# Relation messages added by indirect DMA onto two arrays of sums in DRAM, in place of a target sum stage

## The chip, the core and the metric

The kernel runs on one core of a Trainium2 chip. Its engines work side by side: PE (TensorE: matmuls, and PEld, its weight loads), DVE (VectorE), ACT (ScalarE), POOL (GpSimd) and SP (SyncE, which here only issues DMAs). Each takes its own instructions in order and waits on semaphores that others raise. The metric is the device time of one execution in microseconds (us), the median of three runs.

## The reference

Four graph layers on the same 1250 nodes (768 features, fp32) and 20000 edges, each followed by a residual sum and a layer norm. The first is three graph attentions side by side and an output product W_out, the second a convolution, the third an attention layer. The change touches the fourth: each edge has one of 34 relations, the rows of the sources are averaged by relation and target, multiplied by the relation's matrix and summed by target; a root product and a convolution follow.

```python
seg = edge_type * n + dst
agg = jax.ops.segment_sum(x[src], seg, num_segments=N_REL * n)
cnt = jax.ops.segment_sum(ones, seg, num_segments=N_REL * n)
mean = agg.reshape(N_REL, n, -1) / jnp.maximum(cnt, 1.0).reshape(N_REL, n, 1)
h1 = jnp.einsum('rni,rio->no', mean, W_rel) + x @ W_root + b_rgcn
xw = h1 @ W_gcn
...
out = jax.ops.segment_sum(xw[src] * norm[:, None], dst, num_segments=n)
out = out + xw * (dinv * dinv)[:, None]
return out + b_gcn
```

Below, the key of an edge is target x 34 + relation: edges of one key go to the same row of `mean`.

## The kernel before

Nodes are held as 10 tiles of 128 rows (1250 of 1280 used), features as 6 pieces of 128. The stages, in order of time:

- **Phase 1** (0 to about 620): x1 = relu(x W_ah), then the three products for attention. Beside it DVE counts the edges' places by prefix sums (PREFIX, with two matmuls on PE for the offsets), and POOL scatters edge records into DRAM by 320 indirect DMAs of 125 records (`scatter`, L767): 160 into dstrec_d, sorted by target, 160 into relrec_d, sorted by relation. A target record has four words, a relation record two (source, key). The target records are read back as `drec`, the relation records as `relrec`. The counts by target and key are made from `drec` with L800.
- **First attention** (att0), then the **W_OUT stage** (about 1101 to 1360): three products of 768x768, one for each third of W_out, each over ten tiles. For a tile PE turns the rows (6 transpositions), ACT copies them (`take`), DVE makes the low part (`low_rows`, L406), PE does 36 matmuls (L298), DVE adds the product to the sum (the z-add, L1443). Fp32 numbers are split in a high and a low part, three products for one. In the third of these products the first norm runs with it.
- Convolution, heads, second attention, W_ROOT (the root product into `hbuf`, the array of h1).
- **Relation stage** (2160 to 3475): the edges, sorted by relation and padded to tiles of 128, make RT = 190 tiles. Functions `pool_rel`, `pe_rel`, `act_rel`, `dve_rel`. For tile k POOL gathers 128 source rows from DRAM into `ct` (L1860), PE turns them (L1886: 6 transpositions against the identity), ACT copies them twice (`take`), POOL subtracts for the low part (L1865), PE multiplies by the relation's matrix (L1898: 36 matmuls of 128x384), ACT empties the product with a scale by 1/count (L1935) and stores it to `msg_d` (L1938). PE stands two turns ahead of the products. DVE splits the next relation's matrix (L1835, L1836) as soon as the last tile of the relation before is done.
- **Target sum stage** (3475 to 3746; `pool_sum`, `pe_sum`, `dve_sum`): POOL gathers the messages from `msg_d` by the target records, four tiles to a group, 49 groups (L1979); DVE makes a one-hot matrix of the targets, PE multiplies by it (L1992), DVE adds into the tile of `hbuf` (L2015). All engines meet before and after it.
- **conv3** (3746 to 3938): h1 W_gcn (turn L324, products L298 again), then the aggregation over the graph.

Nothing reorders the work: each engine's order is the order in which its function issues, the stages are called one after the other in the block of each engine, and SP, ACT and POOL each have queues of DMAs that they issue in that order.

## Time and profile before

| | us |
|---|---|
| median of three runs | 3945.08 (3943.74 to 3946.8) |
| span of the profiled execution | 3937.5 |
| W_OUT stage, first and second third, 20 z-adds | 133.6 |
| relation stage | 1315.2 |
| target sum stage with its meets | 270.8 |

The profiled execution was recorded by the hardware profiler; its span is the time from the first to the last record, and what lies around it in a run's time is not in the trace. A stretch in the views is a window of the span. The granted clock is TensorE's, as a share of full speed (2.4 GHz; 0.50 is 1.2 GHz). PE is busy for 92% of the span, but a stage may be bound by something else; so the stages are to be read apart.

### The profile page before, as it was taken

What the parts mean: (1) busy time and instruction counts of PE and PEld (TensorE: products, weight loads), DVE (VectorE), ACT (ScalarE), POOL (GpSimd) and SP (SyncE); (2) the same over time, 40 slices, a digit from 0 to 9 for tenths busy, and PEclk for the clock granted to TensorE, in tenths of its full rate; (3) what the DMA queues carried; (4) which work ended last, traced back from release to release, by engine and by line L of the source; (5) the groups of instructions that cost most, each with busy time, mean ns of one, the idle gap of its engine ahead of it and who ended that gap; (6) DMA issues with size and microseconds to landing.
All of it is one profiled execution on the core that took longest, in us unless ns stands there. A gap on an engine that the chain in (4) does not pass through costs nothing.

```text
span 3937.5 us, 58219 instructions
## 1 busy us (share of the span) xinstructions
PE 3619.1 (92%) x18463; PEld 2965.8 (75%) x18473; DVE 1958.2 (50%) x2783; ACT 1683.3 (43%) x2911; POOL 1555.4 (40%) x1168
## 2 busy tenths in 40 slices
PE   8998868999988897589989999999999999989998
PEld 4555437999978897333335999999999999965588
DVE  7245788888533635899955333332233331013334
ACT  1113677888832321499981333333333333300021
POOL 3887886666600101000001444444444444357600
PEclk9999998999989998799999999999999999999999
DMA  4343212232232302311014555555555553368901
GB/s 144 90 125 74 46 20 63 74 95 74 78 115 90 123 28 81 108 50 40 34 50 144 198 184 184 173 177 186 184 184 189 179 170 133 112 237 302 284 22 67
DMA packets 176460, 483.10 MB, mean 123 GB/s; under 512 B 40798, under 2 KB 57205, under 8 KB 176342
## 3 DMA queue, kind: packets, MB, share of 16 engines
q1 hardware_dynamic: 87414, 201.95, 15.7%
q0 software_dynamic: 54368, 185.24, 15.2%
q10 hardware_dynamic: 34560, 94.45, 6.8%
q8 instruction: 60, 0.98, 0.1%
q14 instruction: 58, 0.48, 0.0%
HBM read 357.64 MB, written 123.55 MB: 122 GB/s over the span
## 4 chain that ended last, share of the span: by engine, by line
PE 40%; ACT 7%; POOL 5%; issue 3%; DVE 2%; DMA 1%; SPq 0%; POOLq 0%; DVEq 0%; ACTq 0%
PE ps L1898 30%; POOL work L1979 5%; ACT work L1279 4%; PE ps L1886 3%; ACT ps L1270 3%; PE ps L1562 3%; PE ps L306 2%; PE ps L298 1%; DVE work L1101 1%; PE ps L1216 1%; DVE work L1129 0%; ACT work L1289 0%; DMA ct<-x_d 0%; DMA work<-msg_d,ct 0%; PE ps L324 0%
## 5 line engine op out<-in xcount | busy, mean ns | idle before, releaser
L1898 PE MATMUL ps<-wsplit,xsplit 128*128 x6840 | 1238.3, 337 | 2.7 <-DVEq L1838 2.7
L1898 PEld LDWEIGHTS ps<-wsplit,xsplit 128*128 128x128 f32 x6840 | 1182.9, 188 | 2.9 <-issue 2.9
L1835 DVE CAST wsplit<-wplain 128x768 fp32r<-128x768 f32 x204 | 117.3, 575 | 760.8 <-PE ps L1898 745.4
L1865 POOL TENSOR_TENSOR xsplit<-ct,xsplit 128x768 fp32r<-128x768 f32 x190 | 369.3, 1944 | 296.2 <-ACTq L1930 296.2
L1279 ACT ACTIVATE work<-ps,work 128x418 f32<-128x418 f32 x720 | 438.6, 632 | 108.5 <-PE ps L1189 103.2
L1935 ACT ACTIVATE ct<-ps,invs 128x768 f32<-128x768 f32 x190 | 171.5, 902 | 714.3 <-PE ps L1898 714.3
L1226 PE MATMUL ps<-hbuf,work 128*128 128x193 f32 x2400 | 455.8, 328 | 14.8 <-DVE work L1143 13.1
L1226 PEld LDWEIGHTS ps<-hbuf,work 128*128 128x128 f32 x2400 | 408.0, 190 | 42.8 <-issue 16.9
L1270 ACT ACTIVATE ps<-work,lr 128x418 f32<-128x418 f32 x720 | 431.8, 634 | 6.0 <-DMA work<-lrow_d 6.0
L1129 DVE SCALAR_TENSOR_TENSOR work<-work,cnt 128x1250 f32<-128x1250 f32 x240 | 350.0, 1459 | 133.5 <-ACT work L1279 132.8
L1860 POOL DMA_INDIRECT ct<-x_d,relrec x190 | 201.1, 1059 | 457.8 <-PE ps L1886 450.2
L1216 PE MATMUL ps<-work,hbuf 128*65 128x512 f32 x720 | 323.5, 532 | 37.6 <-DVE work L1129 35.8
L298 PE MATMUL ps<-wsplit,xsplit 128*128 128x384 f32 x1800 | 335.7, 344 | 13.1 <-DVE xsplit L406 11.8
L298 PEld LDWEIGHTS ps<-wsplit,xsplit 128*128 128x128 f32 x1800 | 321.2, 194 | 15.5 <-issue 7.5
L1323 POOL DMA_INDIRECT invs<-inv_d,relrec x190 | 281.3, 1480 | 60.0 <-issue 57.6
L1189 PE MATMUL ps<-work 128*128 128x418 bf16 x720 | 247.6, 345 | 31.2 <-DMA work<-shift_d 26.8
L1992 PE MATMUL ps<-work 128*128 128x384 f32 x784 | 257.1, 490 | 12.5 <-DMA work<-msg_d,ct 12.1
L767 POOL DMA_INDIRECT relrec_d<-work x160 | 238.9, 1493 | 48.8 <-issue 48.8
L1836 DVE TENSOR_TENSOR wsplit<-wplain,wsplit 128x768 fp32r<-128x768 f32 x204 | 246.1, 1206 | 7.1
L767 POOL DMA_INDIRECT dstrec_d<-work x160 | 206.0, 1287 | 97.6 <-DVEq L688 49.1
L1992 PEld LDWEIGHTS ps<-work 128*128 128x128 f32 x784 | 149.0, 191 | 120.3 <-issue 15.1
L1796 POOL DMA_DIRECT2D x_d<-work x10 | 5.4, 542 | 565.5 <-DVEq L1761 565.5
(212 smaller groups left out, 4380.5 us busy)
## 6 DMA issues: line engine op xcount, KB each, us to landing
wplain<-in_L_gnn_W_rel SPq DMA_DIRECT2D x34, 2304.0 KB, 9.7
msg_d<-ct ACTq DMA_DIRECT2D x190, 384.0 KB, 2.6
work<-lrow_d SPq DMA_DIRECT2D x47, 625.0 KB, 3.7
feat_d<-work ACTq DMA_DIRECT2D x30, 386.0 KB, 4.1
hbuf<-feat_d SPq DMA_DIRECT2D x60, 193.0 KB, 2.5
gat_d<-work POOLq DMA_DIRECT2D x12, 960.0 KB, 5.2
xplain<-gat_d SPq DMA_DIRECT2D x30, 384.0 KB, 3.1
work<-xa_d SPq DMA_DIRECT2D x27, 384.0 KB, 3.3
```

Of the source, the lines that this page charges most:

```text
L298: last = pe.matmul(ps[:, 4 + 2 * u + h, 0:HALF], x[:, u, c * P:(c + 1) * P], w[:, c * D + h * HALF:c * D + (h + 1) * HALF], start=(q == 0 ...
L767: g.indirect_dma_start(out=(relrec_d, dstrec_d)[which], out_offset=bass.IndirectOffsetOnAxis(addr[:, which, t:t + 1], 0), in_=(relpay[:, t ...
L1129: v.scalar_tensor_tensor(p[:, 0:N], p[:, 0:N], 1.0, cnt3[:, q % NT, 0:N], ALU.min, ALU.mult).then_inc(self.s_p, 1)
L1189: pe.matmul(ps[:, b, 0:c1 - c0], self.ones128, self.crow[h % 2][:, c0:c1], start=False, stop=True, skip_group_check=True).then_inc(self.s_ ...
L1216: last = pe.matmul(ps[0:C + 1, 3 + k, 0:n1 - n0], self.feat(h, s), p[:, n0:n1], start=(s == 0), stop=(s == NT - 1))
L1226: last = pe.matmul(ps[:, self.b0 + b, t * (C + 1):(t + 1) * (C + 1)], p[:, dt * P:(dt + 1) * P], self.feat(h, s), start=(s == 0 and t == 0 ...
L1270: act.activation(ps[:, b, 0:c1 - c0], self.Rb[h % 2][:, c0:c1], ACT.Relu, bias=lr[:, col:col + 1]).then_inc(self.s_relu, 1)
L1279: act.activation(self.p[q % 3][:, c0:c1], ps[:, b, 0:c1 - c0], ACT.Exp, bias=self.l2[:, col:col + 1], scale=1.0 - SLOPE)\
L1323: g.indirect_dma_start(out=invs[:, k:k + 1], out_offset=None, in_=inv_d, in_offset=bass.IndirectOffsetOnAxis(relrec[:, 2 * k + 1:2 * k + 2 ...
L1865: g.tensor_tensor(xlo7[:, k % XW, :], xt7[:, k % 2].rearrange("p c n -> p (c n)"), xhi7[:, k % XW, :].bitcast(F32), ALU.subtract).then_inc ...
L1898: last = pe.matmul(ps[:, 4 + 2 * (u % 2) + h, 0:HALF], x[:, u, c * P:(c + 1) * P], w[:, bass.ds(base + (c * D + h * HALF), HALF)], start=( ...
L1992: last = pe.matmul(ps[:, 2 * (u % 2) + h, 0:HALF], sel8[:, GT * (u % 2) + w, :], mg8[:, GT * u + w, h * HALF:(h + 1) * HALF], start=(w == ...
```

## The change

The messages no longer go to DRAM to be gathered again. Each tile of 128 messages is added by an indirect DMA, with the targets as indices and an addition at the destination, onto one of two arrays of sums in DRAM: acc_d[0] begins as the root product, acc_d[1] as zeros; even tiles go to the one, odd tiles to the other. Two edges of one tile with the same key may not both be added by one DMA; therefore the turn of a tile multiplies by a matrix of equal keys (1 where two rows have the same key) in place of the identity, so that each such row holds the sum, and of equal rows all but one are sent to a spare row behind the nodes (`target`, third word of the relation record). Which rows have an equal key behind them is found in 48 rounds of four tiles in the W_OUT stage: POOL compares the keys of a tile with the keys of all its rows and multiplies by the triangle, DVE reduces and writes the target. In the relation stage POOL makes the equality matrix once more for each tile.

```diff
         def pool_same(g, step):
+            def load(b):
+                g.dma_start(key_rows[:, b % 2, :], key_batch(b)).then_inc(s_keyin0[b % 2], 16)
...
+            for b in range(KEY_BATCHES):
+                k0, k1 = batch(b)
+                if b:
+                    g.wait_ge(s_later, b)
+                if k1 < RT:
+                    load(b + 1)
+                g.wait_ge(s_keyin0[b % 2], 16 * (b // 2 + 1))
+                for w in range(k1 - k0):
+                    step.count(g.tensor_scalar(same0[:, w, :], key_rows[:, b % 2, w * P:(w + 1) * P], keys[:, k0 + w:k0 + w + 1], None, ALU.is_equal))
+                step.wait()
+                found = same0[:, 0:k1 - k0, :]
+                g.tensor_tensor(found, found, tri[:, :].unsqueeze(1).to_broadcast([P, k1 - k0, P]), ALU.mult).then_inc(s_same0, 1)
+
+        def dve_target(v, step, b):
+            k0, k1 = batch(b)
+            later, target = small[:, 48:48 + k1 - k0], rel3[:, k0:k1, 2]
+            v.wait_ge(s_same0, b + 1)
+            step(v.tensor_reduce(later, same0[:, 0:k1 - k0, :], AX, ALU.max))
+            v.sem_inc(s_later, 1)
+            step(v.scalar_tensor_tensor(target, later, dummy_row, target, ALU.mult, ALU.max))
+
+        TARGETS = {(l, j): 3 if j < 6 else 2 for l in range(2) for j in range(NT) if l or j}
...
         def dve_wout(v, step):
                     if j + 2 < NT:
                         d.low_rows(v, (j + 2) // 2, j % 2)
+                    for b in TARGET_OF.get((l, j), ()):
+                        dve_target(v, step, b)
...
         def pool_rel(g, step):
+            def equal(k):
+                b, w = divmod(k, KB)
+                if w == 0:
+                    g.wait_ge(s_keyin[b % 2], 16 * (b // 2 + 1))
+                if k >= GW:
+                    g.wait_ge(s_turn7, k - GW + 1)
+                g.tensor_scalar(same7[k % GW], key_rows[:, b % 2, w * P:(w + 1) * P], keys[:, k:k + 1], None, ALU.is_equal).then_inc(s_same7, 1)
+
+            def add(k):
+                g.wait_ge(s_msg7, k + 1)
+                g.indirect_dma_start(out=acc_d[k % 2], out_offset=bass.IndirectOffsetOnAxis(relrec[:, REC * k + 2:REC * k + 3], 0),
+                                     in_=msg7[:, k % 2, :], in_offset=None, compute_op=ALU.add).then_inc(s_msgst[k % 2], 16)
...
+            for j in range(NT):
+                g.wait_ge(W_ROOT.emptied, W_ROOT.b["emptied"] + j + 3)
+                g.dma_start(acc_d[0][j * P:(j + 1) * P, :], hbuf[:, j * D:(j + 1) * D]).then_inc(s_acc0, 16)
+            g.wait_ge(s_acc0, 16 * NT)
             for k in range(RT):
                 if k + GW < RT:
                     gather(k + GW)
+                if k + 2 < RT:
+                    equal(k + 2)
+                if k >= 3:
+                    add(k - 3)
                 low(k)
...
         def pe_rel(pe):
                 for c in range(KC):
-                    last = pe.transpose(ps[:, 2 * (u % 2) + c // 3, (c % 3) * P:(c % 3 + 1) * P], rows7[:, u % GW, 0, c * P:(c + 1) * P], ident[:, :])
+                    last = pe.matmul(ps[:, 2 * (u % 2) + c // 3, (c % 3) * P:(c % 3 + 1) * P], rows7[:, u % GW, 0, c * P:(c + 1) * P],
+                                     same7[u % GW], start=True, stop=True)
...
         def act_rel(act, step):
                 act.wait_ge(s_prod7, k + 3)
-                act.wait_ge(s_msgst[u % 2], 16 * stores)
+                if stores is not None:
+                    act.wait_ge(s_msgst[u % 2], 16 * stores)
...
-                act.dma_start(msg_d[bass.ds(k * P, P), :], msg7[:, u % 2, :]).then_inc(s_msgst[u % 2], 16)
+                act.sem_inc(s_msg7, 1)
```

At the end of the relation stage SP waits until all adds have landed and loads the two arrays of sums tile by tile, two tiles in flight; DVE adds them (`dve_h1`) into `hbuf`, and conv3's turn of a tile waits for that. `pool_sum`, `pe_sum`, `dve_sum` and their two meets are gone. W_gcn is loaded and split as a 35th matrix of the relations. In phase 1 the relation record gets its third word, the target record loses its fourth, the prefix sums by target come first and the target records are scattered first (their addresses are raised on their own), SP clears acc_d[1] and the spare rows with three DMAs (4.7 MB) from a cleared `ct`, and ahead of the W_OUT stage PE turns the keys, and ACT stores them as rows (`pe_keys`, `act_keys`).

On PE, at the start of the relation stage: `ct` holds the gathered rows, `ident` the identity, L1886 is the turn. Before:

```order
L306 MATMUL ps<-mask,ct 128x384 x24
L1886 MATMUL ps<-ident,ct 128x128 x12
L1907 UNCONDITIONAL_BRANCH
L1907 ISA
L1884 ISA
L1886 MATMUL ps<-ident,ct 128x128 x6
```

and now, where L2057 is the turn (its matrix of equal keys lies in `xplain` or `ct`):

```order
L310 MATMUL ps<-mask,ct 128x384 x24
L2057 MATMUL ps<-xplain,ct 128x128 x12
L2079 UNCONDITIONAL_BRANCH
L2079 ISA
L2053 ISA
L2055 REGISTER_ALU
L2057 MATMUL ps<-ct 128x128 x6
```

The six calls of a turn stand where they stood; the operand ident is replaced.

On DVE, at the first tiles of the W_OUT stage (L1443 the z-add, L406 the low rows; in brackets the semaphores waited for). Before:

```order
L1427 RECIPROCAL dinv<-dinv 128x10 [waits degree_roots]
L1443 TENSOR_TENSOR hbuf<-ps,hbuf 128x768 [waits dense_product,wout_bias_in,dve_step]
L406 TENSOR_TENSOR xsplit<-xplain,xsplit 128x768 [waits dve_step,dense_product,dense_taken]
L1443 TENSOR_TENSOR hbuf<-ps,hbuf 128x768 [waits dense_product,wout_bias_in]
L406 TENSOR_TENSOR xsplit<-xplain,xsplit 128x768 [waits dve_step,dense_product,dense_taken]
```

and now (L1545 the z-add, L410 the low rows, L1409 and L1411 a round's end):

```order
L1545 TENSOR_TENSOR hbuf<-ps,hbuf 128x768 [waits dense_product,wout_bias_in]
L410 TENSOR_TENSOR xsplit<-xplain,xsplit 128x768 [waits dve_step,dense_product,dense_taken]
L1409 TENSOR_REDUCE small<-xplain 128x4 [waits equal_keys_marked]
L1411 SCALAR_TENSOR_TENSOR relrec<-small,relrec 128x4 [waits dve_step]
L1409 TENSOR_REDUCE small<-xplain 128x4 [waits equal_keys_marked,dve_step]
L1411 SCALAR_TENSOR_TENSOR relrec<-small,relrec 128x4 [waits dve_step]
L1409 TENSOR_REDUCE small<-xplain 128x4 [waits equal_keys_marked,dve_step]
L1411 SCALAR_TENSOR_TENSOR relrec<-small,relrec 128x4 [waits dve_step]
L1545 TENSOR_TENSOR hbuf<-ps,hbuf 128x768 [waits dense_product,wout_bias_in,dve_step]
L410 TENSOR_TENSOR xsplit<-xplain,xsplit 128x768 [waits dve_step,dense_product,dense_taken]
```

Three rounds now stand between the low rows of a tile and the z-add of the next.

On POOL, inside the relation stage, one tile before (L1860 the gather, L1865 the low part) and the round ahead of the products in the W_OUT stage, which had nothing:

```order
L1860 DMA ct<-x_d,relrec 128x768 x3
L1860 DMA ct<-x_d,relrec 128x768 [waits turned7]
L1865 TENSOR_TENSOR xsplit<-ct,xsplit 128x768 [waits taken7]
L1860 DMA ct<-x_d,relrec 128x768 [waits turned7]
L1865 TENSOR_TENSOR xsplit<-ct,xsplit 128x768 [waits taken7]
```

and now a tile of the relation stage (L1998 the gather, L2014 the compare, L2020 the add, L2003 the low part):

```order
L1998 DMA ct<-x_d,relrec 128x768 [waits turned7]
L2014 TENSOR_SCALAR xplain<-drec,lr 128x128 [waits turned7]
L2020 DMA acc_d<-ct,relrec 1408x768 [waits messages_ready7]
L2003 TENSOR_TENSOR xsplit<-ct,xsplit 128x768 [waits taken7]
L1998 DMA ct<-x_d,relrec 128x768 [waits turned7]
```

The compare and the add of an earlier message stand between a tile's gather and its low part. In the W_OUT stage POOL now has the rounds (L1384 the load of keys, L1397 the compares, L1400 the product by the triangle):

```order
L1384 DMA drec<-keyrow_d 128x512 [waits later_keys_found]
L1397 TENSOR_SCALAR xplain<-drec,lr 128x128 [waits key_rows_in_first1]
L1397 TENSOR_SCALAR xplain<-drec,lr 128x128 x3
L1400 TENSOR_TENSOR xplain<-xplain,tri 128x512 [waits pool_step]
L1384 DMA drec<-keyrow_d 128x512 [waits later_keys_found]
```

Each load, and with it the compares behind it, waits for DVE's reduction of the round before.

## Rows read from the trace of the kernel before

**Rows 1.** The page: the span, and the chain of waits by line.

```profile
span 3937.5 us, 58219 instructions
...
PE ps L1898 30%; POOL work L1979 5%; ACT work L1279 4%; PE ps L1886 3%; ACT ps L1270 3%; PE ps L1562 3%; PE ps L306 2%; PE ps L298 1%; DVE work L1101 1%; PE ps L1216 1%; DVE work L1129 0%; ACT work L1289 0%; DMA ct<-x_d 0%; DMA work<-msg_d,ct 0%; PE ps L324 0%
```

**Rows 2.** Stretches: us, busy (x) of PE PEld DVE ACT POOL, granted clock, DMA share, GB/s.

```profile
1140.42:1273.98 133.56, 126.15 (x750) 124.51 (x747) 52.19 (x60) 42.53 (x119) 1.12 (x2) 0.97 0.23 74
2160.24:3475.40 1315.16, 1315.13 (x7962) 1308.37 (x7962) 356.55 (x407) 454.00 (x563) 561.81 (x373) 1.00 0.50 171
3475.40:3746.15 270.75, 257.11 (x784) 149.01 (x785) 80.77 (x98) 0.90 (x1) 193.12 (x196) 0.98 0.89 295
```

**Rows 3.** Timeline (start, duration, instruction), PE in the relation stage, one tile.

```profile
2300.73 0.82 PE L1886 MATMUL ps<-ident,ct 128*128 128x128 f32 x6
2301.30 6.51 PE L1898 MATMUL ps<-wsplit,xsplit 128*128 x36
2307.66 0.82 PE L1886 MATMUL ps<-ident,ct 128*128 128x128 f32 x6
```

**Rows 4.** L1246, plain fp32 products: two stretches, and durations min/median/max in ns.

```profile
1624.50:1626.50 2.00, 2.00 (x11) 2.00 (x11) 0.50 0.00 0
1627.00:1627.50 0.50, 0.50 (x7) 0.50 (x7) 1.00 0.00 0
...
L1246 PE MATMUL ps<-ident,lr x20: 274/421/581, 1624.0 to 1627.6; 128*128 128x128 f32 x20
```

**Rows 5.** Durations by line: POOL's operations, and DVE's reduction.

```profile
L1865 POOL TENSOR_TENSOR xsplit<-ct,xsplit x190: 1826/1844/2400, 2156.7 to 3459.1; 128x768 fp32r<-128x768 f32 x190
L739 POOL TENSOR_SCALAR_AFFINE_SELECT tri<-ones x1: 294/294/294, 2.1 to 2.1; 128x128 f32<-128x128 f32 x1
L500 DVE TENSOR_REDUCE lr<-work x80: 954/954/957, 151.0 to 1622.8; 128x768 f32 x60, 128x4 f32<-128x768 f32 x20
```

**Rows 6.** Timeline of the W_OUT stage: z-adds, a handoff to POOL.

```profile
1154.24 0.96 DVE L1443 TENSOR_TENSOR hbuf<-ps,hbuf 128x768 f32<-128x768 f32 x1 [2.72 <-PE ps L298]
...
1161.16 0.96 DVE L1443 TENSOR_TENSOR hbuf<-ps,hbuf 128x768 f32<-128x768 f32 x1 [2.74 <-PE ps L298]
...
1298.23 0.68 DVE L449 TENSOR_SCALAR hbuf<-hbuf,small 128x768 f32<-128x768 f32 x1
...
1299.59 0.55 POOL L1469 DMA_DIRECT2D x_d<-hbuf  x1 [28.34 <-DVEq L1459]
```

**Rows 7.** DMA issues: count, KB each, median us from issue to landing.

```profile
msg_d<-ct ACTq DMA_DIRECT2D x190, 384.0 KB, 2.6
...
xplain<-gat_d SPq DMA_DIRECT2D x30, 384.0 KB, 3.1
...
x_d<-work POOLq DMA_DIRECT2D x10, 384.0 KB, 5.3
...
ct<-x_d,relrec POOLq DMA_INDIRECT x190, 4.6
```

**Rows 8.** Timeline: end of the relation stage, end of the target sum stage.

```profile
3475.41 0.90 ACT L1935 ACTIVATE ct<-ps,invs 128x768 f32<-128x768 f32 x1 [5.34 <-PE ps L1898]
...
3745.08 0.96 DVE L2015 TENSOR_TENSOR hbuf<-ps,hbuf 128x768 f32 x1 [5.53 <-PE ps L1992]
...
3746.15 1.53 PE L324 MATMUL ps<-ident,hbuf 128*128 128x128 f32 x12 [1.22 <-DVEq L2016]
```

**Rows 9.** Timeline: DVE and POOL at the split of a relation's matrix.

```profile
2304.11 0.56 DVE L1835 CAST wsplit<-wplain 128x768 fp32r<-128x768 f32 x1
2304.70 2.49 DVE L1836 TENSOR_TENSOR wsplit<-wplain,wsplit 128x768 fp32r<-128x768 f32 x1
...
2307.82 0.96 DVE L1836 TENSOR_TENSOR wsplit<-wplain,wsplit 128x768 fp32r<-128x768 f32 x1
...
2304.35 2.02 POOL L1865 TENSOR_TENSOR xsplit<-ct,xsplit 128x768 fp32r<-128x768 f32 x1 [1.03 <-ACTq L1930]
```

**Rows 10.** DVE's groups by shape: first reader of the target records, waits behind the bar.

```profile
L800 DVE TENSOR_TENSOR hbuf<-iota,drec 128x136 bf16<-128x136 uint16 x49 | 14.7, 301 | 19.2 <-PE ps L844 15.4 <-DVE ct L831 1.4 <-DVE lr L500 0.4
```

More of the change, by code:

```diff
@@ L95, in build @@
         x3_d = dram("x3_d", (NP, D))
[L96 to L97 removed]
+        acc_d = [dram(f"acc{k}_d", (NP + P, D)) for k in range(2)]
+        keyrow_d = dram("keyrow_d", (RT + 2, P), U16)
+        relrec_d = dram("relrec_d", (P * RT, REC), I32)
         dstrec_d = dram("dstrec_d", (P * BT, REC))
@@ new lines, in build, with pe_keys, act_keys @@
+        s_keyin = [sem(f"key_rows_in{u}") for u in range(2)]
+        s_invs = sem("inverse_counts_gathered")
+        def pe_keys(pe):
+            pe.wait_ge(s_keys, 1)
+            pe.transpose(ps[:, 0, HALF:HALF + P], keys0[:, 0:P], ident[:, :])
+            pe.transpose(ps[0:RT + 2 - P, 1, HALF:HALF + P], keys0[:, P:RT + 2], ident[:, :]).then_inc(s_keyt, 1)
+        def act_keys(act, step):
+            act.wait_ge(s_keyt, 1)
+            step.count(act.activation(key_turned[:, 0:P], ps[:, 0, HALF:HALF + P], ACT.Copy))
+            step(act.activation(key_turned[0:RT + 2 - P, P:2 * P], ps[0:RT + 2 - P, 1, HALF:HALF + P], ACT.Copy))
+            act.dma_start(keyrow_d[0:P, :], key_turned[:, 0:P]).then_inc(s_keyst, 16)
+            act.dma_start(keyrow_d[P:RT + 2, :], key_turned[0:RT + 2 - P, P:2 * P]).then_inc(s_keyst, 16)
@@ L1320, in gather_inverses @@
+        for place, count in TARGETS.items():
+            TARGET_OF[place] = range(at, min(at + count, KEY_BATCHES))
+            at += count
+        assert at >= KEY_BATCHES
         def gather_inverses(g, first, last):
@@ L1565, in pe, with dve @@
                         last.then_inc(self.s_agg, 1)
-            def dve(self, v, step):
+            def dve(self, v, step, rows=None):
                 v.sem_inc(self.s_emptied, 2)
@@ L1854, in dve_rel, with dve_h1 @@
             relation(R - 1, 1)
+            relation(R, 0)
+            v.sem_inc(conv3.s_w, KC)
+        def dve_h1(v, j):
+            v.wait_ge(s_sums[j % 2], 32 * (j // 2 + 1))
+            h = hbuf[:, j * D:(j + 1) * D]
+            v.tensor_tensor(h, h, sums7[:, j % GW, :], ALU.add).then_inc(s_h1, 1)
         def pool_rel(g, step):
@@ L1917, in act_rel @@
         def act_rel(act, step):
+            for b in range(2):
+                act.dma_start(key_rows[:, b, :], key_batch(b)).then_inc(s_keyin[b], 16)
             act_root(act)
@@ L1972, in pool_sum @@
-        def pool_sum(g, step):
-            g.wait_ge(s_idx8, 1)
-            for k in range(BG):
-                if k >= UP:
-                    g.wait_ge(s_sum8, k - UP + 1)
-                for w in range(GT):
-                    t = GT * k + w
-                    g.indirect_dma_start(out=mg8[:, GT * (k % UP) + w, :], out_offset=None, in_=msg_d,
-                                         in_offset=bass.IndirectOffsetOnAxis(rows8[:, t:t + 1], 0)).then_inc(s_g8[t % (UP * GT)], 16)
-            g.drain()
@@ L2059, in _ @@
             sp_rel(sp)
-            meet(sp)
-            conv3.dense.load(sp)
             conv3.sp(sp)
```

283 lines of the change are left out of this document (152 added, 131 removed).

## The prediction, made before the changed kernel ran

> **What bounds the kernel now.** I read the chain of waits first: L1898, the relation products, holds 30% of the span, but L1979, the gathers of the target sum stage, holds 5% [rows 1]. So there are two different stages, and each is read by itself in the stretches [rows 2]. In the relation stage (2160 to 3475) PE is busy for all of its 1315 us at a granted clock of 1.00, while POOL has 562 and DVE 357: whatever PE gets there in addition lengthens the kernel, whatever the others get is free until they wait. The timeline of one tile shows a turn (L1886) and 36 matmuls (L1898), 6.93 us from turn to turn [rows 3]. In the target sum stage (271 us) PE looks busy (257), but it waits on rows: the DMA share is 0.89, against 0.50 in the relation stage. The change strikes out this stage and pays in two others: on PE in the relation stage, and in the W_OUT stage, where DVE has 52 and POOL 1 of 134 us to do [rows 2].
>
> **The target sum stage goes.** From the last message's product (ACT empties it at 3475.41) to conv3's first turn at 3746.15 there are 270.7 us [rows 8]. In their place stands a drain: ACT's emptying 0.90 [rows 8], a handoff to POOL, the last indirect add, SP's two loads, DVE's add and a handoff to PE. DVE's add is the shape of L2015, 0.96, and PE starts 0.11 after it [rows 8]. The loads are 384 KB from DRAM, 3.1 by the load of W_OUT's rows [rows 7]. Each handoff I price at the last. The add itself does not occur in the trace. A gather of the same 128 rows lands after 4.6, a plain store of the same bytes after 2.6 [rows 7]; an add that reads and then writes I take at their sum, 7.2, between 4.6 (it is no dearer than a gather) and 12 (somewhat over twice the dearest plain store here, 5.3 [rows 7]). Sum: 0.9 + 0.1 + 7.2 + 0.5 + 3.1 + 1.0 + 0.1 = 13, with an issue 14. So **-257 us** (-260 to -252). What is late next is conv3's first tile; its weights are split already under the last relation's tiles, a gain, and its first two tiles wait for two pairs of sums instead of none, a loss; both are a few us at most and I take 0.
>
> **The turn becomes a product.** Six transpositions against ident become six fp32 matmuls against an equality matrix. A transposition takes between 0.095 (0.57 from the turn's first start to the first L1898, by six) and 0.137 (0.82 to the end of the last, by six) [rows 3]. The plain fp32 product of 128 columns does occur: L1246 makes 10 calls, which the trace shows as 20 instructions [rows 4], two for each. A stretch counts also what began before it and still runs, and these last 0.27 at the least and 0.42 in the median. At a clock of 1.00 seven stand in 0.50 us: (0.50 + 0.27) / 7 = 0.110 from one to the next. At 0.50 eleven stand in 2.00: (2.00 + 0.42) / 11 = 0.22, or 0.110 at the full clock. So one of these instructions costs what a transposition does, and a turn has twelve in place of six: six more of 0.109 are +0.65 on each of 190 tiles, all on PE's path, **+124 us**. Bounds: 0.095 by the starts gives +108, and the longest of L1246 (0.58) in place of the median 0.117, +134.
>
> The Trainium skill ("TensorE: Matmul & The Clock Gate", Terms) says that the transpose mode of a matmul is 4x faster for FP32. By it the turn would be 2.62 us and the term +373. L1246's rows speak against it: at half the clock a call of two instructions would need 0.87 by that rule, and 0.44 is what they show.
>
> **The rest of the relation stage.** POOL gets a compare of 128x128 and an add beside its gather and its subtraction: its 562 us by 190 tiles are 2.96 now [rows 2], of which the subtraction has 1.84; the compare adds 0.29 [rows 5] and the add as much as a gather, the other 1.12: 2.96 + 0.29 + 1.12 = 4.4 us of a tile of 7.6, so it hides, and ACT loses a store and gets a load of keys every fourth tile. The new wait is ACT's: emptying message k+2 waits until add k has landed, and behind it in ACT's queue stand the takes that PE waits for. POOL issues add k only after the gather and the compare of the same pass, which wait for a turn (1.31 + 1.12 + 0.29 = 2.7 us after the product of k); the emptying of k+2 is due two tiles, 15.1 us, after it. So a landing of up to 12 us hides and every us above it costs a share of a us a tile. At 7.2 it costs nothing. Ahead of the loop POOL now stores ten tiles of hbuf and waits for them, with subtraction 0 behind: 10 issues of 0.55 run beside W_ROOT, the last one lands 2.6 to 5.3 after its issue [rows 7], and PE waits: **+3** (+1 to +5).
>
> **The W_OUT stage.** This is the disputed term. 48 rounds, each a chain between POOL and DVE over one buffer (same0): DVE's semaphore frees it, POOL issues the next load of keys, makes four compares, waits for them, multiplies 128x512, and DVE reduces; only then does the next round begin. Two or three of them stand in DVE's queue behind each tile of the first two thirds, ahead of the next tile's z-add and low rows, for which PE waits. None is hidden from the next. Prices: DVE to a DMA issue on POOL 0.68 (1298.91 to 1299.59 [rows 6]) or, by PE's 0.11 [rows 8], less: 0.5. The issue 0.55 [rows 6]. Four compares of one input: 0.29 each by the only POOL operation of 128x128 [rows 5], 1.18. The wait for them 0.1, by PE's 0.11. The product: two inputs, median 1.844 for 768 columns, so 1.23 for 512 [rows 5]. Handoff 0.11. The reduction: 0.954 for 768, 0.64 for 512 [rows 5]. Its semaphore 0.1 likewise. Sum **C = 4.4 us**. The small operation that writes the target runs while POOL is at the next round.
>
> 48 x 4.4 = 211 us must pass, over 19 tiles that take 6.92 each now, 131.5 (z-adds at 1154.24 and 1161.16 are 6.92 apart [rows 6]). That is +80. DVE's own z-add (0.96 [rows 6]) and low rows of the same shape lie under POOL's 3.5 us of a round; on tiles 6 to 9 it also splits six pieces of weights, each a cast of 0.56 [rows 9] and a subtraction, which don't fit under it: following the two queues tile by tile with these durations gives +91 in all. The same by C: 42 us for each us of C. Low end: the product of two-byte marks takes half (0.62) and the handoff 0.11, C = 3.4, +49. High end: compares of 0.59, twice the row, C = 5.6, +141.
>
> Beside it lies contention. DVE's L1836, a subtraction of two SBUF inputs, took 2.49 instead of 0.96 when POOL's two-input L1865 ran from 2304.35 to 2306.37 [rows 9]: it ended 0.82 after POOL, as if it had begun when POOL was done. DVE's low rows are of that kind and will meet POOL's compares or product: up to 0.96 on 19 tiles, +18; often the operation falls to the compares or wins. I take +4: **+95**. The Trainium skill ("SBUF — State Buffer", Who interferes with whom) says that a DVE instruction with two SBUF inputs contends with a GpSimd one that reads SBUF, and that the later one is blocked until the other is done. The row agrees; by it alone the full +18 would be due, 3925 in place of 3911.
>
> **Phase 1.** The target records are scattered 48 us earlier, but their first reader (L800) waits for PE and not for records [rows 10], so the gain is 0. A third word in a record and 4.7 MB of zeros beside the first loads cost 0 to 2, **+1**. With the +3 that makes 4.
>
> **Sum.** -257 + 124 + 95 + 4 = **-34 us**. The profiled execution has a span of 3937.5 [rows 1] against a median of 3945.08; the 7.6 lie around the span and stay. Span 3903.5, time **3911**.
>
> **Rivals.**
> (a) *Dear rounds, slower.* At C above 5.2 the W_OUT stage costs 129 and the change gives nothing. It takes compares of 0.49 instead of 0.29. For it: they read two-byte keys and write another type, nothing in the trace shows this operation on POOL, and four stand in each round, so each 0.1 is worth 17 us. Against it: the 0.29 row. With 0.59 and half of the contention: -257 + 124 + 141 + 9 + 4 = +21, 3966. Chance 0.19.
> (b) *Cheap rounds.* C = 3.4: +49, no contention: -80, 3865. Chance 0.12.
> (c) *Late adds.* If an add lands after 20 us instead of 7, ACT's emptying is 8 us late every second tile: 4 us x 190 = +760. For it: a read and a write of DRAM; against: gathers of the same rows land in 4.6 and the DMA share there is 0.50. About 4670. Chance 0.06.
> (d) *A dear turn.* A call of the new turn takes four times the 0.109 of a transposition, not twice: 2.62 us a turn, 1.31 more than I reckon, +249 on 190 tiles, 4160. Against it stands L1246 [rows 4]; for it, that L1246 shows only some twenty instructions. Chance 0.04.
> That the sums would still be made in a stage of their own is excluded: no instruction of it is left.
>
> **How the numbers follow.** The forecast has 0.59: C between 3.7 and 5.0. 0.2% is 7.9 us, about what a measurement of this kernel can tell from no change. *Faster* by more: (b) and nearly all of the forecast, 0.67. *Same*: C from 5.0 to 5.4, the edge of forecast and (a), 0.09. *Slower*: the rest of (a), (c), (d), 0.24. The range reaches from below (b), 3858, to (a), 3966; (c), (d) and the ends beyond (0.17 together) are left out.
>
> **What would show it.** In the profile after: from turn to turn 7.58 us in the relation stage, with PE busy all the time; 13 to 14 us from the last product to conv3's first turn; from one reduction to the next 4.4 us in the W_OUT stage, with PE waiting for DVE there, and the stage from 134 to some 225 us long; ACT never waiting for an add. The forecast is wrong if a compare is far from 0.29, if adds land after more than 12, or if the turn isn't 1.3.

## The result, and the profile after

The changed kernel takes 3978.0 us (median of four runs, 3974.6 to 3981.1), the kernel before 3944.4 beside it: a ratio of 1.0088, 95% interval 1.0073 to 1.0102. It is slower by 34 us; 3911 was forecast, 34 faster. The profiled execution has a span of 3975.1 against 3937.5 [rows 1], +37.6. The page of the changed kernel: span, granted clock of PE in 40 slices, the chain of waits by engine and by line.

```profile
span 3975.1 us, 58893 instructions
...
PEclk9999998999986779987999999999999999999999
...
PE 43%; ACT 7%; DVE 2%; issue 2%; DMA 1%; POOL 0%; SPq 0%; ACTq 0%; DVEq 0%; POOLq 0%
PE ps L2070 30%; PE ps L2057 6%; ACT work L1306 3%; ACT ps L1297 3%; PE ps L1667 3%; PE ps L310 2%; PE ps L302 2%; DVE work L1128 1%; PE ps L1243 1%; DVE work L1156 0%; ACT work L1316 0%; DMA ct<-x_d 0%; PE ps L328 0%; DVE work L1170 0%; PE ps L1216 0%
```

The 5% of the gathers are out of the chain and the turn (L2057) has 6% where L1886 had 3 [rows 1], both as meant. The chain does not show the loss, though; a sign of it is the dip of the granted clock in slices 12 to 15 (about 1093 to 1491), which hold the W_OUT stage, where PE starves. The span is cut at the starts of the same instructions in both traces:

| part of the span | before | after | difference | forecast |
|---|---|---|---|---|
| to the first z-add of the W_OUT stage | 1129.3 | 1139.5 | +10.2 | +1 |
| first to last z-add (30 of them) | 236.2 | 388.1 | +151.9 | +95 |
| to the first turn of the relation stage | 788.7 | 794.6 | +5.9 | 0 |
| to its first product | 6.0 | 8.8 | +2.8 | +3 |
| relation products, to the last emptying | 1315.2 | 1439.3 | +124.1 | +124 |
| to conv3's first turn | 270.7 | 11.9 | -258.8 | -257 |
| to the end | 191.4 | 192.9 | +1.5 | 0 |

Three of the terms came out to 2 us; two early parts cost 66 more than reckoned. The stretches of the W_OUT stage with rounds, of the relation products and of the drain (columns as in [rows 2], whose three stretches these answer to):

```profile
1139.54:1436.45 296.91, 168.64 (x798) 163.57 (x798) 97.60 (x156) 47.46 (x133) 213.24 (x280) 0.73 0.23 61
2330.97:3769.90 1438.93, 1438.93 (x9086) 1438.91 (x9085) 412.71 (x418) 455.44 (x565) 1050.69 (x750) 1.00 0.68 162
3770.24:3782.16 11.92, 0.01 (x1) 0.01 (x1) 0.96 (x1) 0.90 (x1) 1.55 (x1) 0.69 0.57 143
```

In the first row PE is busy for 169 of 297 us at a clock of 0.73, and POOL, which had nothing to do there, is the busiest engine with 213. In the second PE is busy all the time, now for 1439 us, and ACT's emptying waited for products alone (behind the bars: its busy time and the mean of one, then the time it waited and for what):

```profile
L2110 ACT ACTIVATE ct<-ps,invs 128x768 f32<-128x768 f32 x190 | 171.3, 902 | 917.2 <-PE ps L2070 917.2
```

In the drain SP's first load, which waits for the adds, is issued 5.5 us after the last add:

```profile
3771.53 1.55 POOL L2020 DMA_INDIRECT acc_d<-ct,relrec  x1 [4.69 <-ACTq L2113]
3777.04 0.34 SPq L1948 DMA_DIRECT2D hbuf<-acc_d  x1
```

The timeline of the W_OUT stage, DVE, POOL and PE over one tile:

```profile
1201.13 0.96 DVE L1545 TENSOR_TENSOR hbuf<-ps,hbuf 128x768 f32<-128x768 f32 x1
1201.71 3.17 POOL L1397 TENSOR_SCALAR xplain<-drec,lr 128x128 bf16<-128x128 uint16 x4
1202.30 0.96 DVE L410 TENSOR_TENSOR xsplit<-xplain,xsplit 128x768 fp32r<-128x768 f32 x1 [0.21 <-DVE hbuf L1545]
...
1203.31 8.64 PE L302 MATMUL ps<-wsplit,xsplit 128*128 128x384 f32 x36 [7.70 <-DVE xsplit L410]
...
1206.16 0.69 DVE L1409 TENSOR_REDUCE small<-xplain 128x4 f32<-128x512 bf16 x1 [2.91 <-POOL xplain L1400]
...
1207.20 0.59 POOL L1384 DMA_DIRECT2D drec<-keyrow_d  x1 [1.07 <-DVEq L1410]
1207.84 2.35 POOL L1397 TENSOR_SCALAR xplain<-drec,lr 128x128 bf16<-128x128 uint16 x4
1210.28 1.18 POOL L1400 TENSOR_TENSOR xplain<-xplain,tri 128x512 bf16<-128x512 bf16 x1
1211.56 0.69 DVE L1409 TENSOR_REDUCE small<-xplain 128x4 f32<-128x512 bf16 x1 [4.33 <-POOL xplain L1400]
...
1218.03 0.96 DVE L1545 TENSOR_TENSOR hbuf<-ps,hbuf 128x768 f32<-128x768 f32 x1
```

A tile takes 16.9 us from z-add to z-add where it took 6.92 [rows 6]. The three rounds do it: DVE waits 4.3 us for POOL in each (2.9 in the one that overlaps z-add and low rows), and PE waits 7.7 us for DVE's low rows. The lower clock is not on the path of this tile: PE's products, 8.64 us long, end at 1211.95, and the next z-add begins at 1218.03, behind the third round. From one reduction to the next it is 5.40 us (1206.16 to 1211.56): 0.35 from the reduction's end to the load's issue, 0.64 for that, 2.35 for four compares, 0.09, 1.18 for the product, 0.10 and 0.69. A compare took twice what I had taken for it (min, median and max in ns, over all 190):

```profile
L1397 POOL TENSOR_SCALAR xplain<-drec,lr x190: 592/594/1916, 1127.8 to 1434.3; 128x128 bf16<-128x128 uint16 x190
```

Where DVE also splits weights, a round's four compares take longer still, 4.19 us (and the product behind them 1.69):

```profile
1235.65 4.19 POOL L1397 TENSOR_SCALAR xplain<-drec,lr 128x128 bf16<-128x128 uint16 x4
```

### The profile page after: what moved, and what is told of

It is laid out like the page before. It is cut to its first block, busy times and chain, and to the rows that moved or that the text cites. A ratio compares the mean times of both kernels' runs of the same rounds, so it can differ in the third digit from the quotient of the medians.

```text
span 3975.1 us, 58893 instructions
## 1 busy us (share of the span) xinstructions
PE 3529.9 (89%) x18834; PEld 2986.5 (75%) x18835; DVE 1988.5 (50%) x2792; ACT 1683.7 (42%) x2913; POOL 2105.7 (53%) x1655
## 4 chain that ended last, share of the span: by engine, by line
PE 43%; ACT 7%; DVE 2%; issue 2%; DMA 1%; POOL 0%; SPq 0%; ACTq 0%; DVEq 0%; POOLq 0%
PE ps L2070 30%; PE ps L2057 6%; ACT work L1306 3%; ACT ps L1297 3%; PE ps L1667 3%; PE ps L310 2%; PE ps L302 2%; DVE work L1128 1%; PE ps L1243 1%; DVE work L1156 0%; ACT work L1316 0%; DMA ct<-x_d 0%; PE ps L328 0%; DVE work L1170 0%; PE ps L1216 0%
## 5 line engine op out<-in xcount | busy, mean ns | idle before, releaser
L2070 PEld LDWEIGHTS ps<-wsplit,xsplit 128*128 128x128 f32 x6840 | 1180.2, 188 | 0.0
L2110 ACT ACTIVATE ct<-ps,invs 128x768 f32<-128x768 f32 x190 | 171.3, 902 | 917.2 <-PE ps L2070 917.2
L1964 DVE CAST wsplit<-wplain 128x768 fp32r<-128x768 f32 x210 | 125.4, 597 | 854.7 <-PE ps L2070 837.6
L302 PE MATMUL ps<-wsplit,xsplit 128*128 128x384 f32 x1800 | 364.0, 364 | 120.9 <-DVE xsplit L410 120.6
L2003 POOL TENSOR_TENSOR xsplit<-ct,xsplit 128x768 fp32r<-128x768 f32 x190 | 449.0, 2363 | 0.2
L302 PEld LDWEIGHTS ps<-wsplit,xsplit 128*128 128x128 f32 x1800 | 349.7, 210 | 125.6 <-DVE xsplit L410 85.8
L1998 POOL DMA_INDIRECT ct<-x_d,relrec x190 | 208.0, 1095 | 326.8 <-PE ps L2057 322.9
L2020 POOL DMA_INDIRECT acc_d<-ct,relrec x190 | 342.8, 1804 | 59.0 <-issue 32.5
L1423 POOL DMA_INDIRECT invs<-inv_d,relrec x190 | 304.9, 1605 | 67.0 <-issue 57.6
L1965 DVE TENSOR_TENSOR wsplit<-wplain,wsplit 128x768 fp32r<-128x768 f32 x210 | 291.2, 1387 | 7.3
L793 POOL DMA_INDIRECT dstrec_d<-work x160 | 221.3, 1383 | 63.8 <-issue 63.8
L793 POOL DMA_INDIRECT relrec_d<-work x160 | 225.9, 1412 | 48.8 <-issue 48.8
L1216 PEld LDWEIGHTS ps<-work 128*128 128x128 bf16 x720 | 70.2, 98 | 197.0 <-ACT ps L1297 143.4
```

The lines of the kernel that those rows point to most:

```text
L302: last = pe.matmul(ps[:, 4 + 2 * u + h, 0:HALF], x[:, u, c * P:(c + 1) * P], w[:, c * D + h * HALF:c * D + (h + 1) * HALF], start=(q == 0 ...
L793: g.indirect_dma_start(out=(relrec_d, dstrec_d)[which], out_offset=bass.IndirectOffsetOnAxis(addr[:, which, t:t + 1], 0), in_=(relpay[:, t ...
L1216: pe.matmul(ps[:, b, 0:c1 - c0], self.ones128, self.crow[h % 2][:, c0:c1], start=False, stop=True, skip_group_check=True).then_inc(self.s_ ...
L1423: g.indirect_dma_start(out=invs[:, k:k + 1], out_offset=None, in_=inv_d, in_offset=bass.IndirectOffsetOnAxis(relrec[:, REC * k + 1:REC * k ...
L2003: g.tensor_tensor(xlo7[:, k % XW, :], xt7[:, k % 2].rearrange("p c n -> p (c n)"), xhi7[:, k % XW, :].bitcast(F32), ALU.subtract).then_inc ...
L2020: g.indirect_dma_start(out=acc_d[k % 2], out_offset=bass.IndirectOffsetOnAxis(relrec[:, REC * k + 2:REC * k + 3], 0), in_=msg7[:, k % 2, : ...
```

## Experiments

The theory after the result: the 48 rounds, which stand one after the other between DVE and POOL, are the loss of the W_OUT stage, by the compares' price and by the order; and phase 1's 10 us are PE's, which waits for DVE's prefix sums. Times are medians of four runs; each of the three sets ran beside the kernel before on the same chip, where that had 3945.4, 3939.7 and 3942.6, so a few us between runs of two sets are read from their ratios to it.

**The rounds taken away.**

```diff
...
-            load(0)
-            for b in range(KEY_BATCHES):
+            for b in range(0):
...
-                    for b in TARGET_OF.get((l, j), ()):
-                        dve_target(v, step, b)
...
```

> The changed kernel without the 48 rounds of the W_OUT stage (neither the compares and the product on POOL nor the reductions on DVE); the key rows are still made. It leaves out which rows hold an equal key behind them, so all adds go to the 128 spare rows of the sums, one row each. Theory: the rounds are the loss. The W_OUT stage, 152 us longer than before from its first to its last z-add, falls back to its old length, PE's clock there rises again, and the time falls by 150 to 158 us, to 3820 to 3828, some 120 below the kernel before. Rival, the loss in the W_OUT stage comes from the key rows' transfers or from the bias that comes late, not from the rounds: it falls by less than 30.

3823.9 us, 154 less than the changed kernel and 0.9693 of the kernel before (0.9677 to 0.9709). The W_OUT stage in the trace of this run, from first to last z-add:

```profile
1138.20:1375.00 236.80, 212.51 (x1224) 209.51 (x1224) 109.35 (x157) 73.90 (x208) 9.91 (x18) 0.93 0.31 104
```

It is 236.8 us long, 236.2 before. So the rounds are all of the +152, and key rows and bias none of it; the start of the stage stays 9 us late, so that part has another cause. Of the 5.9 us behind the stage nothing is left either (789.0 from the last z-add to the first turn), so they follow from the rounds, too. How stays open: in four of the runs below, in which the stage is shorter than in the changed kernel, this part takes 791 us, and the granted clock of the 100 us behind the stage does not order them (0.95 for 791.0 in the first run with both changes together, 0.97 for 795.9 in the run with halved compares).

**Two buffers for the marks.**

```diff
...
-                if b:
-                    g.wait_ge(s_later, b)
+                if b >= 2:
+                    g.wait_ge(s_later, b - 1)
...
-                    step.count(g.tensor_scalar(same0[:, w, :], key_rows[...
+                    step.count(g.tensor_scalar(same0[b % 2][:, w, :], key_rows[...
...
```

> The changed kernel with two buffers for the marks of equal keys in place of one, so that POOL may make the next round while DVE reduces this one. Theory, the chain: a round of 5.4 us holds POOL's load 0.6, compares 2.4, product 1.2 and then 1.1 to 1.2 of handoffs and the reduction; with two buffers only POOL's part of 4.3 is left, and DVE's queue no longer stands between: at 42 us for each us of a round the time falls by 40 to 55, to 3923 to 3938. Rival, POOL is slowed by DVE's instructions on the same memory so that its own part fills the round: it falls by less than 15.

3913.8 us, 64 less (ratio to before 0.9921, 0.9905 to 0.9938). It gave more than the 40 to 55 of the theory. POOL's round is 4.2 us where nothing disturbs it, as expected, and DVE's z-add, low rows and splits now pass beside it. POOL is the bound:

```profile
1201.17 3.13 POOL L1397 TENSOR_SCALAR xplain<-drec,lr 128x128 bf16<-128x128 uint16 x4
...
1204.38 1.16 POOL L1400 TENSOR_TENSOR xplain<-xplain,tri 128x512 bf16<-128x512 bf16 x1
1205.49 0.59 POOL L1384 DMA_DIRECT2D drec<-keyrow_d  x1
...
1206.12 2.34 POOL L1397 TENSOR_SCALAR iota<-drec,lr 128x128 bf16<-128x128 uint16 x4
1208.55 1.17 POOL L1400 TENSOR_TENSOR iota<-iota,tri 128x512 bf16<-128x512 bf16 x1
```

There is no gap between POOL's instructions, and the four compares again take 3.13 when DVE has its z-add and low rows beside them, 2.34 otherwise. Of the +152 the strict order is thus 61 (the stage has 327.0 us here); the other 91 are left with POOL's own time.

**A compare's price.**

```diff
-                for w in range(k1 - k0):
-                    step.count(g.tensor_scalar(same0[:, w, :], key_rows[:, b % 2, w * P:(w + 1) * P], keys[...
+                for w in range(2 * (k1 - k0)):
+                    h = slice(w % 2 * 64, w % 2 * 64 + 64)
+                    step.count(g.tensor_scalar(same0[:, w // 2, h], key_rows[:, b % 2, w * 64:(w + 1) * 64], keys[...
```

> The changed kernel with each of POOL's compares of 128x128 cut into two of 128x64: the same result, eight instructions a round for four. A compare took 0.594 us where 0.29 was reckoned. Theory, a price for each instruction of about 0.3 beside one for each column (2.3 ns): a half takes 0.45, a round grows by 1.2 us from 5.4 to 6.6, and at 42 to 48 us for each us of a round the time grows by 50 to 58, to 4028 to 4036. Rival, the price is all by the column (4.6 ns): halves take 0.30 and nothing changes, 3974 to 3984.

4019.7 us, +42: under the theory's range, and far from the rival's. The compares in the profile, their row over the whole run and one round from reduction to reduction:

```profile
L1398 POOL TENSOR_SCALAR xplain<-drec,lr x380: 430/431/1706, 1128.9 to 1478.1; 128x64 bf16<-128x64 uint16 x190
...
1202.18 0.69 DVE L1410 TENSOR_REDUCE small<-xplain 128x4 f32<-128x512 bf16 x1 [5.29 <-POOL xplain L1401]
...
1203.86 3.32 POOL L1398 TENSOR_SCALAR xplain<-drec,lr 128x64 bf16<-128x64 uint16 x8
...
1208.53 0.69 DVE L1410 TENSOR_REDUCE small<-xplain 128x4 f32<-128x512 bf16 x1 [5.29 <-POOL xplain L1401]
```

A half takes 0.431 us, a whole 0.594: 0.163 for 64 columns, 2.5 ns each, and 0.27 for the instruction. So the theory's form holds for these two sizes, with a slightly smaller price for the instruction. Eight halves in a row take 3.32 us where four wholes took 2.35, a round goes from 5.40 to 6.35, +0.95 and not the +1.2 expected, and the W_OUT stage grew by 43 us (431.1): 45 us for each us of a round, where the prediction said 42.

**The compares on DVE.**

```diff
...
-                    step.count(g.tensor_scalar(same0[:, w, :], key_rows[...], keys[...], None, ALU.is_equal))
-                g.tensor_tensor(found, found, tri[...], ALU.mult).then_inc(s_same0, 1)
...
+                step.count(v.scalar_tensor_tensor(same0[:, w, :], key_rows[...], keys[...],
+                                                  tri[:, :], ALU.is_equal, ALU.mult))
...
```

> The changed kernel with the compares and the product by the triangle moved from POOL to DVE (four instructions of 128x128, compare and product in one); POOL only loads the key rows. Theory: what a round costs is POOL's arithmetic and the handoffs to it. On DVE four instructions of some 0.2 us, the reduction 0.69, the target 0.22 and three waits of 0.15 make 2.1 to 2.2 a round, and three of them fit nearly beside a tile of 6.92: the W_OUT stage is 10 to 35 us longer than before the change instead of 152, the time 3840 to 3865. Rival, PE's low clock in the starved stage is what costs, and any round in DVE's queue brings it about: over 3900.

3883.2 us, 95 less than the changed kernel (0.9857 of before, 0.984 to 0.9873). Neither range holds it: the stage has 292.6 us, +56 instead of the +10 to +35 expected. A round takes 2.26 us, slightly over the estimate, but with z-add, low rows and a wait of about 1 us for key rows a tile with three takes DVE 9.8 us, not 6.92, and there are eleven such tiles. Such a tile is shown below, in the run with both changes together.

**The turn against the identity.**

```diff
-                    last = pe.matmul(ps[...], rows7[...], same7[u % GW], start=True, stop=True)
+                    last = pe.transpose(ps[...], rows7[...], ident[:, :])
```

> The changed kernel with the turn of the relation stage made against the identity, as six transpositions, in place of six products with the matrix of equal keys, which POOL still makes; equal keys of a tile are thus not summed. Theory: PE bounds the relation stage, and twelve instructions of a turn become six: 6.92 us a tile instead of 7.58, 124 us less, 3854. Rival, POOL with its gather, compare, add and subtraction (6.1 us busy of 7.58 a tile) becomes the bound as soon as PE gets faster: 50 to 100 less, 3880 to 3930.

3849.8 us, 128 less by the medians, 125 of them in the relation products. PE's timeline of a tile in this run and in the changed kernel:

```profile
2400.10 0.82 PE L2057 MATMUL ps<-ident,ct 128*128 128x128 f32 x6
2400.67 6.51 PE L2069 MATMUL ps<-wsplit,xsplit 128*128 x36
2407.03 0.82 PE L2057 MATMUL ps<-ident,ct 128*128 128x128 f32 x6
```

```profile
2407.14 1.50 PE L2057 MATMUL ps<-xplain,ct 128*128 128x128 f32 x12
2408.39 6.49 PE L2070 MATMUL ps<-wsplit,xsplit 128*128 x36
2414.72 1.50 PE L2057 MATMUL ps<-xplain,ct 128*128 128x128 f32 x12
```

6.93 us from turn to turn against 7.58: the step of the prediction on the turn. PE is busy for all of 1310 us of the stage in this run, POOL for 1099: the rival falls. ACT's emptying now waited for an add 34 times (162.2 us in all), without PE losing anything, so the adds hide with less to spare here.

**The prefix matmuls moved behind on PE, first one pair, then both.**

```diff
-                if j == 2 and behind:
+                if j == 0 and behind:
+                    prefixes(0, R, NT)
+                if j == 2 and behind:
                     prefixes(1, 0, R)
-            prefixes(0, R, NT)
```

Both versions move the first pair as shown; the second also moves `prefixes(1, 0, R)` to j == 4.

> The changed kernel with the two matmuls of the target prefix sums moved on PE from ahead of W_AH's first turn to behind its first product. Theory: in phase 1 PE stands 8 to 11 us behind DVE's marks, which POOL's clearing of ct holds up (the ten marks took 13.3 us together); with the matmuls behind, W_AH begins at about 16 us as before, and the time falls by 10 to 12, to 3966 to 3968. Rival, the 4.7 MB of zeros or the third word of the records delay phase 1: no change, 3974 to 3982.

3979.2 us: no change, so the theory fell in this form. PE's waits from 20 to 160 us show why (engine, line, what it waited for, sum, count, longest), first in the changed kernel, then in this run:

```profile
PE ps L621 <- DVEq L671: 24.0, 1, 24.0
```

```profile
PE ps L621 <- DVEq L672: 10.0, 1, 10.0
```

In the changed kernel PE stands at the targets' prefix from the start to 24.0 us; in this run it begins with W_AH at 15.9, as before, but then stands for 10.0 us at the second pair, behind the third product, for the relations' sums that DVE makes last. One wait took the place of the other. In the second version that pair stands behind the fifth product:

> The changed kernel with both pairs of prefix matmuls moved behind on PE: the targets' behind W_AH's first product, the relations' behind the fifth instead of the third. With the first pair alone moved PE began at 15.9 us as before, but then waited 10.0 us for DVE at the second pair. Theory: phase 1's 10 to 11 us are PE's waits on DVE's prefix sums and nothing else; with both moved the time falls by 9 to 12, to 3966 to 3969. Rival, the waits only move on to a third place (the rows of x behind the zeros, ACT): no change, 3975 to 3982.

3965.4 us, 12.6 less by the medians (1.0059 of before, 1.0042 to 1.0076; about 11 by the ratios), and the first z-add is at 1126.6, earlier than the 1129.3 before the change. So PE's two waits account for the whole of phase 1's loss, and nothing is left for the zeros to explain; what they cost by themselves no run shows.

**Both together, and two more steps.** The rounds on DVE, four of them ahead of the first z-add, and both pairs of prefix matmuls behind:

```diff
-        TARGETS = {(l, j): 3 if j < 6 else 2 for l in range(2) for j in range(NT) if l or j}
+        TARGETS = {(l, j): 3 if j < 6 else 1 if j < 8 else 2 for l in range(2) for j in range(NT) if l or j}
+        EARLY = 4
...
                     step(v.reciprocal(dinv[:, :], dinv[:, :]))
+                    for b in range(EARLY):
+                        dve_target(v, step, b)
```

> The changed kernel with the rounds on DVE, four of them ahead of the first z-add (where DVE waits 9.6 us for the bias), three behind each of the tiles 1 to 5 and 0 to 5, one or two behind the tiles at which DVE splits weights; and both pairs of prefix matmuls behind on PE. Theory: -11 of phase 1 and the W_OUT stage within 10 to 25 us of its length before the change: 3825 to 3845, 100 to 120 below the kernel before. Rival, the two parts don't add (phase 1's gain is eaten by a later wait): 3836 to 3860.

3856.6 us (0.9791 of before, 0.9774 to 0.9807). It beats both kernels, but misses its range by 12: the W_OUT stage still has 278.6 us, and the first z-add, behind the four early rounds, comes at 1134.3, 7.7 later than in the run with both pairs moved. The third of these rounds waited for its key rows:

```profile
1129.63 1.26 DVE L1407 SCALAR_TENSOR_TENSOR xplain<-drec,lr,tri 128x128 bf16<-128x128 uint16 x4 [6.74 <-DMA drec<-keyrow_d]
```

So phase 1's gain is in part spent again, as the rival has it, but on the early rounds. DVE over one tile in this run:

```profile
1183.50 0.96 DVE L1549 TENSOR_TENSOR hbuf<-ps,hbuf 128x768 f32<-128x768 f32 x1
1184.66 0.96 DVE L410 TENSOR_TENSOR xsplit<-xplain,xsplit 128x768 fp32r<-128x768 f32 x1 [0.21 <-DVE hbuf L1549]
...
1185.54 1.13 DVE L1407 SCALAR_TENSOR_TENSOR xplain<-drec,lr,tri 128x128 bf16<-128x128 uint16 x4
...
1186.71 0.69 DVE L1410 TENSOR_REDUCE small<-xplain 128x4 f32<-128x512 bf16 x1
1187.55 0.23 DVE L1412 SCALAR_TENSOR_TENSOR relrec<-small,relrec 128x4 int32<-128x4 f32 x1 [0.15 <-DVE small L1410]
...
1191.02 1.14 DVE L1407 SCALAR_TENSOR_TENSOR xplain<-drec,lr,tri 128x128 bf16<-128x128 uint16 x4 [0.99 <-DMA drec<-keyrow_d]
```

The third round of a tile waits 1 us for its key rows. With a third place for them, loads are issued two rounds ahead:

```diff
+        slots0 = [key_rows[:, 0, :], key_rows[:, 1, :], iota[:, 0:KB * P]]
...
-                if k1 < RT:
-                    load(b + 1)
+                if b + 2 < KEY_BATCHES:
+                    load(b + 2)
...
```

> The version with the rounds on DVE and both pairs of prefix matmuls behind (3857 us), with a third place for key rows, so that loads are issued two rounds ahead. DVE waited 19 us in all for key rows, about 1 us at every third round. Theory: in the W_OUT stage DVE bounds (9.8 us for a tile with three rounds of 2.26 and 6.92 for PE), so these waits lie on the path, and the time falls by 9 to 18, to 3839 to 3848. Rival, DVE would have waited for products in any case: no change, 3852 to 3862.

3848.5 us, 0.9762 of the kernel before (0.9746 to 0.9778), 2.4% faster and the best here of the versions that do the whole work. The stage has 266.9 us, 11.7 less. By the medians the gain is 8, but these were taken on two chips; by the ratios (0.9791 and 0.9762) it is about 11, in the theory's 9 to 18, and the rival falls.

In the last run the odd rounds go back to POOL, ahead of DVE and into a buffer of their own, and three rounds instead of four stand ahead of the first z-add:

```diff
+            if b % 2:
+                v.wait_ge(s_same0, b // 2 + 2)
+            else:
                 for w in range(k1 - k0):
                     step.count(v.scalar_tensor_tensor(same0[:, w, :], slots0[b // 2 % 2][...], keys[...], tri[:, :], ALU.is_equal, ALU.mult))
...
```

> As the run with three places, but POOL compares and multiplies for every second round into a buffer of its own, ahead of DVE, and DVE does the other rounds in full; DVE reduces all. Theory: DVE's work for a tile with three rounds falls from 9.8 us to about 7 to 8, near PE's 6.92; the W_OUT stage comes within 5 to 20 us of its length before the change, the time to 3825 to 3842. Rival, DVE's compares (two SBUF inputs) and POOL's hold each other up, so that POOL's rounds come late (over 6 us for two rounds): 3845 to 3870, no better than DVE alone.

3858.4 us, 10 slower than DVE alone: the rival's time. A round of POOL's comes every 6.4 to 6.9 us, and in the stage DVE waits 18.7 us for POOL's marks, a wait that the run before does not have, while its own work there falls only from 198 to 190 us; the difference comes near the 10. The timeline shows what slows the two engines:

```profile
1183.48 2.22 DVE L410 TENSOR_TENSOR xsplit<-xplain,xsplit 128x768 fp32r<-128x768 f32 x1 [0.22 <-DVE hbuf L1566]
1183.72 1.16 POOL L1406 TENSOR_TENSOR iota<-iota,tri 128x512 bf16<-128x512 bf16 x1
...
1186.70 1.29 DVE L1424 SCALAR_TENSOR_TENSOR xplain<-drec,lr,tri 128x128 bf16<-128x128 uint16 x4
1186.72 2.52 POOL L1401 TENSOR_SCALAR iota<-iota,lr 128x128 bf16<-128x128 uint16 x4 [1.32 <-DMA iota<-keyrow_d]
...
1192.80 4.06 POOL L1401 TENSOR_SCALAR iota<-iota,lr 128x128 bf16<-128x128 uint16 x4 [0.95 <-DMA iota<-keyrow_d]
...
1193.11 1.00 DVE L402 TENSOR_TENSOR wsplit<-wplain,wsplit 128x768 fp32r<-128x768 f32 x1
...
1197.78 1.43 POOL L1406 TENSOR_TENSOR iota<-iota,tri 128x512 bf16<-128x512 bf16 x1
1198.10 2.04 DVE L1424 SCALAR_TENSOR_TENSOR xplain<-drec,lr,tri 128x128 bf16<-128x128 uint16 x4
```

Where the two sets of compares meet, each loses little: 2.52 instead of 2.35 on POOL, 1.29 instead of 1.14 on DVE. POOL's compares take 4.06 beside DVE's split of weights (L402). Beside POOL's product by the triangle DVE's compares take 2.04, and its low rows 2.22 instead of 0.96: the low rows end 0.82 us after the product, as the split of [rows 9] ended 0.82 after POOL's subtraction.

## Why the prediction was wrong, point by point

- **The target sum stage goes, -257:** right, -258.8. The drain is 11.9 us; an add takes 6.1 from issue to landing in the median (5.2 to 11.0), where I took 7.2, and the last one at most 5.5. The sum of a gather and a store was somewhat dear, and the path was right.
- **The turn, +124:** right, +124.1, and with the identity 125 of them come back in the relation products. A tile takes 7.58 us, as forecast to the digit. (The 0.117 of the upper bound is what the longest row of L1246 gives, not a median.) The rival with a turn of four times falls: by the starts a turn goes from 0.57 to 1.25 us. The Trainium skill ("TensorE: Matmul & The Clock Gate", Terms) says that the transpose mode is 4x faster for FP32; taken against a plain fp32 product, as in the prediction, the run against the identity shows a factor of about 2 for this shape.
- **Adds hide in the relation stage, 0:** right. ACT's emptying waited only for products there (917.2 us, 190 times, none for an add), and the rival of late adds falls. POOL is busier than reckoned, 1051 of 1439 us, or 5.5 a tile instead of 4.4: in the mean an add's issue takes 1.80, not 1.12, a compare 0.82, not 0.29, and the subtraction 2.36, not 1.84 (they overlap in part). It still hides, by less than it looked.
- **Start of the relation stage, +3:** right, +2.8.
- **The W_OUT stage, +95:** wrong, +151.9; this is the step that failed. The mechanism was right, as the run without rounds shows, and so, nearly, was the conversion, 45 us measured for a us of a round against 42. Two terms of the sum were mis-sized. (1) *The round:* 5.40 us, not 4.42. The compares are 2.35, not 1.18; the rest is 3.05, not 3.24. I took the price from the one POOL operation of 128x128 in the trace (0.294, [rows 5]), of another kind and other types, and it was not a bound. At 42 us, +0.98 are +41. (2) *Contention:* in 18 rounds POOL's compares ran beside work of DVE. Nine of them, beside the z-add and the low rows, took 3.17 instead of 2.35, and four, beside a split of weights, about 4.2 with a longer product; over all 18 the excess adds up to some 21, where I took 4 of the 18 us that I had as an end. 91 + 41 + 21 = 153 against 152; the parts overlap where DVE splits weights, so the sum is no proof to the us. The sentence from the Trainium skill ("SBUF — State Buffer", Who interferes with whom) that I weighed and did not follow, +18 by it, came nearer than my choice; in the trace POOL was the one that was slowed, though, not DVE's low rows, which took 0.96.
- **Phase 1, +1:** wrong, +10.2 at the first z-add, and the runs with the matmuls behind give 11 to 13 back. I looked at the scatter and at the zeros, but not at what the moved prefix matmuls do on PE: they stand ahead of all of its work and wait for DVE. A move was priced on the engine it was meant for, not on the queue it stands in.
- **From the W_OUT stage to the relation stage, 0:** wrong by 5.9, which are gone without the rounds; the cause stays open.

Rival (a), dear rounds, is what happened: compares of 0.59 and half of the contention gave 3966; phase 1 is most of what it lacked to 3978, so the range ended 12 us too low. I gave it 0.19; a price that stands in no row, times 190, should have had more.

## What to carry to other kernels

A serial chain between two engines that is put into a third one's loop, and is longer than the loop's own work (here 48 rounds of 5.4 us against 19 tiles of 6.92), sets the loop's length, so its price must be known to a tenth of a us: here each 0.1 us of a compare, 190 times, was worth some 17 us, and the only row like it was of another operation. Where the nearest row is not the same operation and types, the forecast should lean to the dear end, and a change that gains 250 us at one place and pays at four should be priced as four unknowns. When an instruction that waits is moved to the head of an engine's queue, ask first what that engine would have done in the meantime; and when one wait is taken away, look for the second that stands behind it, as here at 10.0 us.

## What the runs showed of the hardware

- A compare on POOL (u16 in, bf16 out) took 0.594 us for 128 columns and 0.431 for 64, by these two 0.27 us for the instruction and 2.5 ns for a column; on DVE a compare with a product by a second matrix in one instruction takes 0.347 by the profile and four in a row 1.14, 0.285 each. The two engines sharing the rounds, in the one arrangement tried, were slower than DVE alone.
- The changed kernel's ten marks on DVE (of 125x160) stood beside POOL's clearing of ct and ended 0.7 us after it; one of them shows 11.56 us, where the median is 0.23. Before, the same ten had taken 1.61, after POOL's clearing was done. The rows, the changed kernel's first:

```profile
6.66 13.31 DVE L662 TENSOR_SCALAR hbuf<-work 125x160 f32<-125x160 f32 x10
...
8.20 11.08 POOL L770 MEMSET ct<- 128x13140 uint16 x1
```

```profile
13.98 12.62 POOL L750 MEMSET ct<- 128x13140 uint16 x1 [6.83 <-DMA dstrec_d<-hbuf]
...
27.49 1.61 DVE L651 TENSOR_SCALAR hbuf<-work 125x160 f32<-125x160 f32 x10
```

  That POOL's clearing held them is not tested by a run of its own.
- An indirect add of 128 rows of 3 KB onto DRAM lands after 6.1 us in the median while gathers of rows of that size land after 4.1 in the same trace, and its issue holds POOL for 1.6 us (median).
